# Vision tower with routed experts, one core: the product down with tokens as weights, its result in rows in one bank

## What is computed

```python
for e in range(E):
    h = jax.nn.gelu(tokens @ w1[e] + b1[e], approximate=False)
    y = h @ w2[e] + b2[e]
    out = out + combine[:, e:e + 1] * y
...
h = _layernorm(h + ffn(h), axis=-1)
```

## Time and profile before

| | us |
|---|---|
| median of 3 runs | 855.12 (854.82 to 855.29) |
| the profiled execution | 855.08 |
| its span | 853.0 |
| TensorE busy | 838.5 (98%) |
| VectorE busy | 781.0 (92%) |
| ScalarE busy | 660.0 (77%) |
| GpSimd busy | 184.8 (22%) |

### The profile page before, as it was taken

How to read it: one execution, slowest core, us unless ns; L and a number is a source line. 1 busy time by engine, 2 the same in 40 slices (tenths; PEclk the granted TensorE clock), 3 DMA queues, 4 the chain that set the end, 5 groups by cost and what they waited for, 6 DMA issues and landing times.

```text
span 853.0 us, 31799 instructions
## 1 busy us (share of the span) xinstructions
PE 838.5 (98%) x13818; PEld 431.9 (51%) x13818; DVE 781.0 (92%) x920; ACT 660.0 (77%) x1312; POOL 184.8 (22%) x191
## 2 busy tenths in 40 slices
PE   9999999999999999999999999999999999999995
PEld 6444556755555555555555555555555555543331
DVE  4888999999999999999999998999989999999994
ACT  0368888888888888888888888888888888977873
POOL 1275910000400000000000000000000299948323
PEclk9999999999999999999999999999999999999998
DMA  9982150000000000000000000000000000000111
GB/s 297 348 219 59 27 91 3 3 2 2 3 3 3 3 2 3 2 3 2 2 3 2 3 3 3 3 2 3 3 2 3 3 3 3 3 2 2 39 26 37
DMA packets 31578, 26.09 MB, mean 31 GB/s; under 512 B 12552, under 2 KB 29456, under 8 KB 31440
## 3 DMA queue, kind: packets, MB, share of 16 engines
q1 hardware_dynamic: 22912, 15.54, 7.5%
q10 hardware_dynamic: 8464, 8.52, 3.2%
q0 software_dynamic: 64, 0.01, 0.0%
HBM read 17.77 MB, written 2.10 MB: 23 GB/s over the span
## 4 chain that ended last, share of the span: by engine, by line
PE 89%; DVE 6%; DMA 2%; issue 2%; ACT 1%; POOLq 0%; DVEq 0%; POOL 0%; ACTq 0%
PE ps L565 37%; PE ps L582 26%; PE ps L595 12%; PE ps L668 3%; PE ps L752 3%; DVE ring L1101 3%; DMA big<-in_x_dram 2%; PE ps L609 1%; PE ps L473 1%; PE ps L681 1%; PE ps L487 1%; PE ps L767 1%; PE ps L449 0%; DVE ring L1266 0%; DVE sums L1060 0%
## 5 line engine op out<-in xcount | busy, mean ns | idle before, releaser
L1101 DVE TENSOR_TENSOR ring<-ring 128x1024 f16<-128x1024 f32 x512 | 605.0, 1233 | 33.1 <-ACT ring L974 32.1
L974 ACT ACTIVATE ring<-ps 128x1024 f32<-128x1024 f32 x512 | 519.7, 1021 | 120.7 <-PE ps L565 120.5
L565 PE MATMUL ps<-big 64*64 64x512 f16 x6144 | 376.1, 375 | 1.3 <-ACT ring L974 0.9
L582 PE MATMUL ps<-ring,both_f 64*64 64x512 bf16 x4096 | 275.1, 384 | 0.0
L565 PEld LDWEIGHTS ps<-big 64*64 64x64 f16 x6144 | 176.6, 106 | 160.3 <-ACT ring L974 5.5
L582 PEld LDWEIGHTS ps<-ring,both_f 64*64 64x64 f16 x4096 | 119.3, 106 | 106.6
L595 PE MATMUL ps<-ring,both_f 64*64 64x512 f16 x2048 | 154.3, 376 | 0.1
L974 ACT ACTIVATION_READ_ACCUMULATOR ring<-ps 128x1 f32 x512 | 101.3, 198 | 0.0
L393 POOL TENSOR_SCALAR stat<-stat 128x16 f32<-128x16 f32 (+2 forms) x4 | 2.9, 723 | 444.0 <-DVE stat L1150 443.7
L595 PEld LDWEIGHTS ps<-ring,both_f 64*64 64x64 f16 x2048 | 59.8, 107 | 51.8 <-issue 1.9
L937 ACT ACTIVATE ring<-ps,b1s 128x512 f32<-128x512 f32 x64 | 40.4, 683 | 16.7 <-PE ps L668 16.6
(11 more groups left out here) (193 smaller groups left out, 550.4 us busy)
## 6 DMA issues: line engine op xcount, KB each, us to landing
ring<-in_x_dram ACTq DMA_DIRECT2D x6, 1024.0 KB, 15.4
ring<-in_x_dram SPq DMA_DIRECT2D x6, 1024.0 KB, 21.7
big<-big SPq DMA_DIRECT2D x16, 128.0 KB, 2.4
out_dram<-h SPq DMA_DIRECT2D x14, 128.0 KB, 2.4
both_f<-in_x_dram ACTq DMA_DIRECT2D x1, 1024.0 KB, 22.0
both_f<-in_x_dram SPq DMA_DIRECT2D x1, 1024.0 KB, 22.3
big<-in_x_dram SPq DMA_DIRECT2D x1, 1024.0 KB, 24.1
big<-in_x_dram ACTq DMA_DIRECT2D x1, 1024.0 KB, 14.6
```

The lines of the kernel that those rows point to most:

```text
L565: last = mm(bank(SLOT_BANK[slot_of(s)] + r)[m:m + 64, :], of_k[r][:, 128 * k + m:128 * k + m + 64], of_q[r][:, q0 + 512 * r:q0 + 512 * r + ...
L582: last = mm(bank(sums_bank(s // NT) + half)[m:m + 64, :], fs[64 * r:64 * r + 64, s % NT, m:m + 64], probs[64 * r:64 * r + 64, s % 8, :].bi ...
L974: a(probs[:, s % 8, :], bank(SLOT_BANK[slot_of(s)], 2), ACT.Exp, accum_out=rowsum[:, s:s + 1]).then_inc(s_pr, 1)
L1101: tt(probs_lo[:, s % 8, :], probs[:, s % 8, :], probs[:, s % 8, :].bitcast(BF16)[:, 1:2 * QC:2], ALU.subtract).then_inc(s_lo, 1)
```

## The change

The product down takes 64 weighed tokens as weights and w2 as the moving operand: for each pair of experts 16 matmuls of 64 x 64 (4 column groups p, 2 halves r, 2 halves m of the array) in place of two of 512 columns. The result then has tokens in rows and features in columns, as h has, and is added up over the four pairs in one bank: bank 4 for even blocks, bank 5 for odd ones, bank 7 for the second half of the last block. The bias is put in in the same way, with 64 columns of the router's weights as weights. The transposes, ScalarE's copy, `yT` and `s_yev` go. VectorE's addition waits for the last product down of the block (`s_dn`), and in the last block its first piece for half of it (`s_y`). The first product down of a block waits for the addition of the block two before. In the last two blocks additions, squares and variance of block NG - 2 come one step earlier.

```diff
-        def result_bank(w):
-            return bank(7) if w == NG else bank(5)
+        def result_bank(z, p):
+            return bank(7) if z == NG - 1 and p >= TP // 2 else bank(4 + z % 2)
...
             def down(u):
                 y, i = u // NPAIR, u % NPAIR
...
-                if i == 0 and y >= 1:
-                    pe.wait_ge(s_yev, y)
-                pe.wait_ge(s_hw, 2 * u + 2)
-                if i == 0:
-                    for n in range(2):
-                        mm(bank(4)[64 * n:64 * n + 64, :], b2s[:, n, :], combT[:, y % 2, :],
-                           start=True, stop=False, skip_group_check=True)
-                for n in range(2):
-                    last = mm(bank(4)[64 * n:64 * n + 64, :], w2s[:, i, :], hidc[:, (2 * u + n) % 4, :],
-                              start=False, stop=(i == NPAIR - 1), skip_group_check=True)
-                last.then_inc(s_dn, 1)
-            def result(w):
-                z, p0, p1 = PIECES[w]
-                pe.wait_ge(s_yev, w + 1)
...
-                for p in range(p0, p1):
-                    last = mm(result_bank(w)[:, 128 * p:128 * p + 128], yT[:, z % 2, 128 * p:128 * p + 128], ident,
-                              is_transpose=True, start=True, stop=True)
-                last.then_inc(s_y, 1)
+                if i == 0 and y >= 2:
+                    pe.wait_ge(s_z, y - 1)
+                if i == 0 and y == NG - 1:
+                    pe.wait_ge(s_centred, NG)
+                pe.wait_ge(s_hw, 2 * u + 2)
+                def tile(p, r, m):
+                    return result_bank(y, p)[m:m + 64, D * (2 * p + r):D * (2 * p + r) + D]
+                if i == 0:
+                    firsts = (0, TP // 2) if y == NG - 1 else (0,)
+                    for p in range(TP):
+                        for r in range(2):
+                            for m in (0, 64):
+                                mm(tile(p, r, m), combT[:, y % 2, 128 * p + m:128 * p + m + 64], b2s[:, r, :],
+                                   start=(p in firsts and r == 0), stop=False, skip_group_check=True)
+                for p in range(TP):
+                    for r in range(2):
+                        for m in (0, 64):
+                            last = mm(tile(p, r, m), hidc[:, (2 * u + r) % 4, 128 * p + m:128 * p + m + 64], w2s[:, i, :],
+                                      start=False, stop=(i == NPAIR - 1), skip_group_check=True)
+                    if u == NPAIR * NG - 1 and p == TP // 2 - 1:
+                        last.then_inc(s_y, 1)
+                last.then_inc(s_dn, 1)
...
# ScalarE
-                    if i == 0 and z >= 0:
-                        for w in pieces_of(z):
-                            result_out(w)
...
-                    if i == 3 and z >= NG - 2:
+                    if 0 <= z and i == {NG - 2: 2, NG - 1: 3}.get(z):
                         for w in pieces_of(z):
                             out_squares(w)
...
# VectorE
-                dve.wait_ge(s_y, w + 1)
+                if w == NG - 1:
+                    dve.wait_ge(s_y, 1)
+                else:
+                    dve.wait_ge(s_dn, NPAIR * z + NPAIR)
...
+                    if i == 3 and z == NG - 2:
+                        for w in pieces_of(z):
+                            final_variance(w)
                     if u < NPAIR * NG:
                         weigh(u, 0)
                         weigh(u, 1)
...
-                    if 0 <= z and i == (2 if z >= NG - 2 else 3):
+                    if 0 <= z and i == {NG - 2: 1, NG - 1: 2}.get(z, 3):
                         for w in pieces_of(z):
                             result_added(w)
...
-                    if i == 3 and z >= NG - 2:
+                    if i == 3 and z == NG - 1:
                         for w in pieces_of(z):
                             final_variance(w)
```

More of the change, by code:

```diff
@@ L217, in tower @@
         late = ring[:, 0:15 * 512].rearrange("p (i t) -> p i t", t=512)
-        hid, hidc, yT = late[:, 0:4], late[:, 4:8], late[:, 8:10]
+        hid, hidc = late[:, 0:4], late[:, 4:8]
         sq_o = late[:, 13, :].rearrange("p (j o) -> p j o", o=D)
@@ L256, in tower @@
         (s_mean, s_hc, s_hcsq, s_vh, s_at, s_spc, s_spq, s_cr, s_vs, s_cov, s_den, s_n2, s_inv, s_var, s_istd, s_ab, s_scaled, s_of_s, s_ln,
-         s_htr, s_htev, s_lg, s_gap, s_route, s_centred, s_tanh, s_comb, s_ctr, s_cev, s_up, s_gelu, s_ex, s_hw, s_dn, s_yev, s_y, s_z,
+         s_htr, s_htev, s_lg, s_gap, s_route, s_centred, s_tanh, s_comb, s_ctr, s_cev, s_up, s_gelu, s_ex, s_hw, s_dn, s_y, s_z,
          s_osq, s_var2, s_istd2, s_fin, s_out) = (sem(n) for n in (
@@ L260, in tower @@
              "s_istd", "s_ab", "s_scaled", "s_of_s", "s_ln", "s_htr", "s_htev", "s_lg", "s_gap", "s_route", "s_centred", "s_tanh",
-             "s_comb", "s_ctr", "s_cev", "s_up", "s_gelu", "s_ex", "s_hw", "s_dn", "s_yev", "s_y", "s_z", "s_osq",
+             "s_comb", "s_ctr", "s_cev", "s_up", "s_gelu", "s_ex", "s_hw", "s_dn", "s_y", "s_z", "s_osq",
              "s_var2", "s_istd2", "s_fin", "s_out"))
@@ L785, in _ @@
                         sums_tokens(NQ - 1, i)
-                    if i == 1 and g >= 1:
-                        for w in pieces_of(g - 1):
-                            result(w)
                     if i == 2 and g + 2 < NG:
@@ L916, in combine_out @@
                 a(combT[:, g % 2, :], bank(6).bitcast(F16)[:, 0:BLK], ACT.Copy).then_inc(s_cev, 1)
-            def result_out(w):
-                z, p0, p1 = PIECES[w]
-                act.wait_ge(s_dn, 4 * z + 4)
-                if z == 0:
-                    act.wait_ge(s_ph, NC // 2)
-                    act.wait_ge(s_lo, NS)
-                if z >= 2:
-                    act.wait_ge(s_y, z - 1)
-                a(yT[:, z % 2, 128 * p0:128 * p1], bank(4)[:, 128 * p0:128 * p1], ACT.Copy).then_inc(s_yev, 1)
             def out_squares(w):
@@ L1270, in result_added @@
                 t = slice(G * z + 2 * p0, G * z + 2 * p1)
[L1271 to L1272 removed]
+                if w == NG - 1:
+                    dve.wait_ge(s_y, 1)
+                else:
+                    dve.wait_ge(s_dn, NPAIR * z + NPAIR)
+                stt(h[:, t, :], h[:, t, :], 2.0, result_bank(z, p0)[:, 128 * p0:128 * p1].rearrange("p (j o) -> p j o", o=D),
                     ALU.mult, ALU.add).then_inc(s_z, 1)
```

7 lines of the change are left out of this document (1 added, 6 removed).

## The result

| | before | with the change |
|---|---|---|
| median, 19 runs each | 855.29 us | 853.86 us |
| ratio | | 0.9984 (95%: 0.9977 to 0.9991) |
| the same again, later: medians | 855.59 us | 853.40 us |
| ratio | | 0.9975 (0.9965 to 0.9985) |
| span of the profiled execution | 853.0 us | 851.8 us |

The last row of the table leaves that out: the tail is **1.94 us** shorter.

What follows compares the result with a forecast made beforehand. Middle blocks of the tail were taken as bound by VectorE's own chain, 10.98 us, so worth 0; blocks 6 and 7 (-0.43) and the end (-1.13) gave -1.56 us on the 853.0 us span: 851.4, plus 2.08 around it, 853.5 us; range 852.8 to 855.2.

Steps and rivals of the forecast that it cites:

- the bound of what can be told: Whole kernel: about 0.2% (1.7 us) is what a measurement can tell from no change.
- Product down: Each of a block's four downs on TensorE: +0.07 to +0.13 us, priced by the sums of tokens, 32 records in 1.08 us.
- a load and a stream follow each other: Rival, TensorE's product down: weight loads and streams run one after another, a down 2.0 us, about 885 us; 2%.
- instructions run short: Rival, tail: instruction supply stops at 36.7 TensorE records per us, a block takes 12.4 us, kernel 863 us; 6%.
- Bias: Once a block on TensorE: 16 matmuls of 64 columns take 0.47 us, +0.23 us; bounds 0.24 and 0.52 us.
- Middle blocks: Six middle blocks of the tail: worth 0 us, bounds 0 and +0.3 us, period staying at VectorE's 10.98 us.
- the predicted cover: TensorE's product down ahead of the router weights' transposes: old wait 0.12 us, cover ends at 1.03 us, 1.00 taken.
- The reason given for it: Middle block: VectorE's own chain, 12 instructions x 0.60 us plus 16 of some 0.24 us, is the period, 10.98 us.
- TensorE as the bound: Rival, middle blocks: a down over 1.03 us ahead of the router weights' transposes makes TensorE the bound, about 854.5 us; 14%.
- ScalarE's copy: ScalarE's copy of the result, 0.66 us: nobody waits for it in middle blocks, so its time there is only room.
- Blocks 6 and 7: Last two blocks: bias step gives 0.25 us each, one down gives back 0.07; last product down starts 0.43 us sooner.
- The end: From last product down to VectorE's second addition: 2.37 us becomes 1.24, gain 1.13 us; GpSimd's cover 1.5 us.

Runs made afterwards that it cites:

- the run with the old order: Changed kernel with block 6's squares, addition and variance put back one step later; ratio 0.9989 against the kernel before, tail 101.90 us.
- the run with scaling ahead of the addition: Interleaved kernel (changed kernel, VectorE's long instructions between router steps) with VectorE's scaling of h before the addition; 852.64 us, ratio 0.9972 against the kernel before.
- the interleaved run: Changed kernel with normed, a second weighing and the variance placed between VectorE's router steps; ratio 0.9977 against the kernel before, tail 100.66 us.

## Why the prediction was right, and where its reason was not

The forecast was 853.5 us, 0.19% faster and just inside the bound of what can be told; measured were 853.86 us and 0.16%, then 853.40 us and 0.25%. By its steps:

- *Product down.* Taken as 1.08 us before another tile shape and 1.00 before the same, bounds 0.98 and 1.08; measured 1.06 to 1.08 and 0.98. The sums of tokens were the right row. The rivals that a load and a stream follow each other and that instructions run short are refuted (a product of 32 records in 1.06 us; 46.6 records per us). With the first falls, for this case, the sentence of the Trainium skill (TensorE: Matmul & The Clock Gate, Part 3, "The mechanism") that the prediction weighed: loads of the same row group do overlap matmuls here. The two column halves take turns, and no run shows whether the overlap is between the halves or within one.
- *Bias.* **The mis-sized term.** Taken as 0.47 us, nearest to the router scores' eight pairs; measured 0.27, close to the low bound of 0.24. The router scores are 8 float32 matmuls, each recorded twice, the bias is 16 matmuls of 16 bits, recorded once: 16 records either way, in 0.52 and in 0.27 us. So the count was right and the type was left out; a short 16-bit record cost half of a float32 one, which none of the numbered rows showed. It made blocks 6 and 7 gain 0.45 us each in the step with the bias instead of 0.25.
- *Middle blocks.* Forecast 0 us, measured 0.00 to 0.01 us a block. Right, and the predicted cover is there: the wait ahead of the router weights' transposes shrank from 0.12 to 0.05 us. Not predicted is where the bias's step went: 0.28 us of its 0.45 come back as a wait for the weighings one step later.
- *The reason given for it* ("VectorE's own chain is the period") holds only in part. A shorter TensorE doesn't help, as stated (half of the product left out: 10.97 us). But the period is the loop of router, transposes, product up, GELU, weighing; VectorE's sum is level with it, and taking 0.60 us off VectorE outside the loop gives 0.03 us (`scaled` left out), while 0.47 us inside it gives 0.41. The sum 12 x 0.60 + 16 x 0.24 came out at 10.98 partly because the 0.24 us had been worked out from the period itself.
- *TensorE as the bound.* Given 14% with a margin of 0.03 us. TensorE's own sum was 10.56 us and not 10.94: 0.20 us of the difference is the bias, the rest 0.02 us in its step and 0.03 to 0.07 us in each of the other three, whose old lengths I had carried over whole. The margin was 0.10 us in each of four steps. Two prices given there don't follow from their own working: two downs longer by 16 x 10 ns are 0.32 us a block and 1.9 us in six, so 855.4 and not 856; at 6 ns the same gives 854.7, not the 855.2 of the range's end.
- *ScalarE's copy,* "worth nothing but room": right in these two kernels, whose middle blocks are equally long, and the room is worth up to 0.4 us a block once the order on VectorE is changed (up to, because the products differ too).
- *Blocks 6 and 7.* Forecast 2 x 0.25 - 0.07 = 0.43 us, measured 0.75. The bias gives 2 x 0.20 more; against that, the plain step behind block 6's bias was taken to stay at 2.48 us and became 2.59 (826.64 to 829.23), since the expansion waits for the weighings there too.
- *The end.* Forecast 1.13 us, measured 1.17. That GpSimd would be late without the earlier variance was shown directly by the run with the old order: 1.24 us lost, about all of the gain at the end. With it GpSimd was free at 842.65 + 1.04 = 843.69 and needed at 845.11, a cover of 1.42 us where 1.5 was forecast.

Together the tail became 1.94 us shorter against 1.56 forecast, and of the 0.38 us more 0.32 are in blocks 6 and 7 and 0.04 at the end. The median of the first series still lies 0.36 us above the forecast and that of the second 0.10 below it: whole runs spread by more than the terms do (851.99 to 857.78 us in the first series).

## What to carry to other kernels

Where an engine is busy all the time, ask of each of its instructions whether it lies between a release and the work that leads to that release again: only there did a shorter instruction shorten the period; leaving one out tells it. A change that shortens the chain behind the last product has to be followed to the next engine in it, since here over half of the gain needed one block's addition, squares and variance moved by a step, which by itself was worth nothing. When an operation is priced by a neighbour, use one of the same type: 16 short records took 0.27 us at 16 bits and 0.52 us in float32, and a float32 matmul has two of them.

## What the runs showed of the hardware

A VectorE instruction with two operands in the SBUF and GpSimd's scaling of h (128x512, read from the SBUF) exclude each other, and the later one waits in its duration, not in a gap: VectorE's 0.22 us became 1.00, 0.36 became 1.12, 0.68 became 1.15 beside GpSimd's scaling of 1.04 us, and that scaling became 1.43 to 1.51 us where VectorE came first. GpSimd's small steps held nothing up, long as they last: beside the one with 8 columns (L428, 1.63 us from 807.73 in the run with scaling ahead of the addition) VectorE's L1245 (807.82) kept its 0.36 us, and beside one with 24 columns (L417, 4.19 us from 779.40 in the interleaved run) VectorE's L1146 (782.63) kept its 0.68 us. The Trainium skill (SBUF — State Buffer, "Who interferes with whom") states this exclusion for any GpSimd instruction that reads the SBUF. The rows of the scaling agree with it, those of the small steps don't, and one meeting with the scaling a block was enough to undo a better order.

A recorded load and matmul with 64 columns cost about 0.03 us in TensorE's stream in float32 (16 in 0.51 us, 32 in 0.98 us, two records a matmul) and 0.017 us at 16 bits (16 in 0.27 us, one record a matmul). In float32 the number of records set the price more than the columns did, since 16 records of the router scores, with 16 columns each, took 0.52 us. At 16 bits no run tells the two apart: the 0.27 us are close to the 0.24 us in which the same columns streamed before.
